# Cross-attention and gated FFN on one core: the V projection made straight behind K, the first half of U ahead of tile 2's scores, and inputs laid out by partition

## What is computed

```
q = (layernorm(x) @ Wq) * s ; k = (context @ Wk) * s ; v = context @ Wv        # s = 128 ** -0.25
attn = softmax(q @ k.T, per head) ; x = x + (attn @ v) @ Wo + bo
n = layernorm(x) ; shared = relu(n @ Ws1)**2 @ Ws2
logits = n @ Wr ; rw = softmax(top 2 of logits) ; prob = trunc(rw placed on the experts)
routed = sum over experts of prob * (relu(n @ W1[e])**2 @ W2[e])
x = x + shared + routed
```

## Time and profile before

| what | value |
|---|---|
| median of 3 runs | 116.21 us |
| the profiled execution | 116.54 us |
| its span, first to last instruction | 114.7 us |
| PE busy | 109.2 us (95%) |
| DVE, ACT, POOL busy | 87.6, 85.9, 65.5 us |
| PE's granted clock, mean | 0.996 |
| read from HBM, written | 8.42 MB, 2.10 MB |

### The profile page before, as it was taken

The page is one execution under the profiler, slowest core; times in us unless marked ns, Lnnn a source line. Parts: engine busy times, 40 slices in busy tenths (PEclk is TensorE's granted clock), DMA queues, the critical chain, the costliest instruction groups (busy, mean ns, idle before and its releaser), DMA issues.

```text
span 114.7 us, 3118 instructions
## 1 busy us (share of the span) xinstructions
PE 109.2 (95%) x854; PEld 105.8 (92%) x854; DVE 87.6 (76%) x349; ACT 85.9 (75%) x349; POOL 65.5 (57%) x106
## 2 busy tenths in 40 slices
PE   6987999999999989999999999999999999999991
PEld 6975999899998989999999999999999999989980
DVE  1019888569889697797979797987979786979973
ACT  4006926997948979898988889898989888997330
POOL 2005735956372965785676578657856766259341
PEclk9999999999999999999999999999999999999998
DMA  2899999995000200031005000400400050013034
GB/s 55 256 334 364 357 352 352 348 348 184 1 6 0 91 0 3 6 130 53 0 0 183 0 0 24 159 0 0 150 33 0 0 183 3 0 61 122 0 137 137
DMA packets 11815, 12.70 MB, mean 111 GB/s; under 512 B 1056, under 2 KB 10272, under 8 KB 11808
## 3 DMA queue, kind: packets, MB, share of 16 engines
q1 hardware_dynamic: 11520, 12.36, 32.4%
q10 hardware_dynamic: 288, 0.26, 0.7%
HBM read 8.42 MB, written 2.10 MB: 92 GB/s over the span
## 4 chain that ended last, share of the span: by engine, by line
PE 76%; DVE 7%; ACT 6%; DMA 4%; SPq 2%; issue 2%; POOL 1%; ACTq 0%; DVEq 0%
PE o_ps L432 8%; PE o_ps L434 7%; PE o_ps L433 7%; PE s_ps L432 7%; PE s_ps L434 7%; PE s_ps L433 7%; PE g_ps L492 6%; DMA wqt_sb<-in_wq_t 4%; PE f_ps L522 4%; ACT probs L710 4%; PE g_ps L505 3%; PE f_ps L432 2%; PE g_ps L446 2%; PE s_ps L622 1%; DVE wq_mean L1079 1%
## 5 line engine op out<-in xcount | busy, mean ns | idle before, releaser
L710 ACT ACTIVATE probs<-s_ps,neg_max,rstd 128x77 f32<-128x77 f32 x112 | 45.4, 428 | 4.0 <-DVE neg_max L950 4.0
L840 POOL TENSOR_TENSOR probs<-probs,recip 128x308 f32<-128x308 f32 x27 | 19.0, 703 | 23.5 <-DVE recip L956 23.4
L710 ACT ACTIVATION_READ_ACCUMULATOR probs<-s_ps,neg_max,rstd 128x1 f32 x112 | 24.2, 216 | 0.0
L432 PE MATMUL o_ps<-u_hi,pt_hi 128*128 128x256 f32 (+1 forms) x80 | 22.7, 284 | 0.2 <-DVE pt_lo L961 0.2
L434 PE MATMUL o_ps<-u_lo,pt_hi 128*128 128x256 f32 (+1 forms) x80 | 22.4, 280 | 0.0
L433 PE MATMUL o_ps<-u_hi,pt_lo 128*128 128x256 f32 (+1 forms) x80 | 22.4, 280 | 0.0
L432 PE MATMUL s_ps<-a_hi,xt_hi 128*128 128x308 f32 x64 | 22.1, 345 | 0.0
L434 PE MATMUL s_ps<-a_lo,xt_hi 128*128 128x308 f32 x64 | 19.4, 303 | 0.0
L433 PE MATMUL s_ps<-a_hi,xt_lo 128*128 128x308 f32 x64 | 19.4, 303 | 0.0
L432 PEld LDWEIGHTS o_ps<-u_hi,pt_hi 128*128 128x128 f32 (+1 forms) x80 | 15.0, 188 | 0.6 <-DVE pt_lo L961 0.6
L433 PEld LDWEIGHTS o_ps<-u_hi,pt_lo 128*128 128x128 f32 (+1 forms) x80 | 15.1, 188 | 0.0
(11 more groups left out here) (190 smaller groups left out, 270.8 us busy)
## 6 DMA issues: line engine op xcount, KB each, us to landing
xt_sb<-in_x_t SPq DMA_DIRECT2D x8, 256.0 KB, 6.7
x_sb<-in_x SPq DMA_DIRECT2D x8, 256.0 KB, 6.7
x_sb<-x_tr SPq DMA_DIRECT2D x7, 256.0 KB, 2.3
out<-y_sb SPq DMA_DIRECT2D x6, 256.0 KB, 2.3
wqt_sb<-in_wq_t SPq DMA_DIRECT2D x4, 256.0 KB, 5.0
wo_sb<-in_wo SPq DMA_DIRECT2D x1, 1024.0 KB, 9.0
wk_sb<-in_wk_p SPq DMA_DIRECT2D x3, 256.0 KB, 3.1
wv_sb<-in_wv_p SPq DMA_DIRECT2D x2, 384.0 KB, 6.2
```

What stands on the lines that cost most here:

```text
L432: pe.matmul(out_ap, hi, rhs_hi, start=first, stop=False)
L710: e = act.activation(probs_of(t)[:, par, h * TK:(h + 1) * TK], s_ps[:, 2 * par + half, (h - half * H // 2) * TK:(h - half * H // 2 + 1) * TK],
L840: pool.tensor_tensor(rows, rows, recip[:, par, hs].unsqueeze(2).broadcast_to([P, H // 2, TK]), ALU.mult).then_inc(probs_ready, 1)
```

## The change

Three things are changed. On PE, V's products stand straight behind K's, before A; half of U's products (heads 0 to 3) stand ahead of tile 2's scores, the other half behind them; and the first of U's transposes stands ahead of tile 0's transposition. ACT's and DVE's copies follow that order. On SP, Wv is loaded ahead of Wq. And the inputs are laid out by partition on the host, so that most loads read one piece of 2, 4 or 8 KB for each partition where they read pieces of 1 to 3 KB, and there are fewer loads: 21 in place of 32.

```diff
-            for i in range(2):
-                sp.dma_start(wk_sb[:, i, 0:HG, :].rearrange("p e c -> p (e c)"), wk_p[:, i, 0:HG * P]).then_inc(wk_in[i], 16)
...
+            def load_context_weights(w_sb, w_p, main_in, tail_in):
+                sp.dma_start(w_sb[:, 0:H, :], w_p[:, 0:H, :]).then_inc(main_in, 16)
+                sp.dma_start(w_sb[:, H:WT, :], w_p[:, H:WT, :]).then_inc(tail_in, 16)
...
+            sp.dma_start(ctx_sb[:, :, :], ctx_p).then_inc(ctx_in, 16)
+            load_context_weights(wk_sb, wk_p, wk_in, wk_tail_in)
+            load_context_weights(wv_sb, wv_p, wv_in, wv_tail_in)
             for i in range(4):
-                load_wq(i)
...
+                sp.dma_start(wqt_sb[:, 2 * i:2 * i + 2, :], wq_p[:, 2 * i:2 * i + 2, :]).then_inc(wq_in[i], 16)
             load_x_t(0)
             load_x(0)
...
-            load_wv(0)
-            load_wv(1)
...
@@ A: heads 4 to 7 write the banks that V's copies free @@
                     if h < H // 2:
                         pe.wait_ge(kt_copied, h + 1)
+                    else:
+                        pe.wait_ge(vt_copied, h - H // 2 + 1)
...
@@ PE's order @@
+            context_main(wk_sb, wk_in, s_banks)
+            context_tails(wk_sb, wk_tail_in, s_banks, kt_ready)
+            context_main(wv_sb, wv_in, once_banks)
+            context_tails(wv_sb, wv_tail_in, once_banks, vt_ready)
             make_a()
...
             scores(1, 1)
-            pe.wait_ge(wsr_ready, 1)
-            for i in range(2):
-                context_main(wv_sb, i, wv_in[i], once_banks)
-            context_tails(wv_sb, once_banks, vt_ready)
+            make_ut(0, H // 2)
             scores(2, 0)
-            make_ut()
+            make_ut(H // 2, H)
             pe.wait_ge(const_ready, 4)
+            make_u(0, 0)
             pe.wait_ge(exp_done, 5)
             transposes_x1(0, 0, transposes(0, 0))
-            for b, i in ((0, 0), (1, 0), (0, 1), (1, 1)):
+            for b, i in ((1, 0), (0, 1), (1, 1)):
...
@@ DVE @@
+            keep_ut(0)
+            keep_ut(1)
             reciprocals(0, 0, 0)
+            keep_ut(2)
+            keep_ut(3)
             reciprocals(0, 0, 1)
             maxima(2, 0)
             neg_maxima(2, 0)
...
+            reciprocals(1, 1, 0)
+            for h in range(4, H):
+                keep_ut(h)
+            reciprocals(1, 1, 1)
+            lo_of_u(0, 0)
             lo_of_transposes(0, 0)
```

More of the change, by code:

```diff
@@ L65, in program @@
     HALFP = P // 2
-    assert WB == HG + 2 and HG == 4
+    assert WT == H + 4 and HG == 4
     PB = (KC - 1) * P
@@ L396, in _, with context_main, context_tails @@
         def _(pe):
-            def context_main(w, i, w_in, banks):
+            def context_main(w, w_in, banks):
                 pe.wait_ge(w_in, 16)
-                for j in range(HG):
-                    h = HG * i + j
-                    pe.matmul(banks[h // 2][:, (h % 2) * BK:(h % 2 + 1) * BK], w[:, i, j, :], ctx_sb[:, 0, :],
+                for h in range(H):
+                    pe.matmul(banks[h // 2][:, (h % 2) * BK:(h % 2 + 1) * BK], w[:, h, :], ctx_sb[:, 0, :],
                               start=h % 2 == 0, stop=False)
-            def context_tails(w, banks, ready):
+            def context_tails(w, w_in, banks, ready):
+                pe.wait_ge(w_in, 16)
                 for i in range(2):
@@ L434, in three, with make_ut @@
                 return pe.matmul(out_ap, hi, rhs_lo, start=False, stop=last)
-            def make_ut():
-                for h in range(H):
+            def make_ut(first, end):
+                for h in range(first, end):
                     if h == 0:
                         pe.wait_ge(wo_in, 16)
-                    if h < H // 2:
-                        pe.wait_ge(vt_copied, h + 1)
-                    else:
+                    if h == 0:
+                        pe.wait_ge(wsr_ready, 1)
+                    if h >= H // 2:
                         pe.wait_ge(ut_copied, h - H // 2 + 1)
@@ L740, in _ @@
                                ACT.Copy, scale=SCALE2).then_inc(kt_copied, 1)
-                if g == 0:
-                    centre_wq(0, 2)
+            centre_wq(0, 2)
+            for g in range(H // 2):
+                act.wait_ge(vt_ready, g + 1)
+                act.activation(vt_sb[:, 2 * g:2 * g + 2, :].rearrange("p h n -> p (h n)"), once_banks[g][:, 0:2 * BK],
+                               ACT.Copy).then_inc(vt_copied, 1)
             centre_wq(4, 8)
@@ L751, in _ @@
             exps(0, 0, 1)
-            for g in range(H // 2):
-                act.wait_ge(vt_ready, g + 1)
-                act.activation(vt_sb[:, 2 * g:2 * g + 2, :].rearrange("p h n -> p (h n)"), once_banks[g][:, 0:2 * BK],
-                               ACT.Copy).then_inc(vt_copied, 1)
             exps(1, 1, 0)
@@ L758, in _ @@
             exps(2, 0, 0)
+            hi_of_u(0, 0)
             copy_transposes(0, 0)
-            for b, i in ((0, 0), (1, 0), (0, 1)):
+            for b, i in ((1, 0), (0, 1)):
                 hi_of_u(b, i)
@@ L1131, in _ @@
             step(1, 1, TG)
[L1132 to L1133 removed]
+            dve.wait_ge(x_in[2], 16)
+            dve.wait_ge(x_in[3], 16)
             with dve.Fori(1, (TILES - TG) // 2) as j:
```

111 lines of the change are left out of this document (45 added, 66 removed).

## The result

The changed kernel took 117.18 us (median of 20 runs, 116.62 to 118.13) against 116.44 (20 runs of the kernel before on the same chip): ratio 1.0074, 95% interval [1.0057, 1.0092]. It is slower by 0.7%, and outside the range of 115.4 to 116.8. The profiled execution took 117.23 us with a span of 115.4; 116.40 was forecast for it. All ratios leave out executions more than 1.5% above the fastest of the same kernel: one of experiment 5, three of experiment 10, and two of the kernel before beside experiments 9 and 10.

The account below looks back on a forecast made before the run. PE's stream was taken as the bound, capped by ACT: PE gains 1.95 us but gets 1.8 us of new waits; transposition +0.30, one transpose group -0.44, together -0.14 us, median 116.1 us. Range 115.4 to 116.8.

Parts of the forecast that it names:

- it stays there if the Wk load is there: Start of PE's work: K's first pass stays at 4.78 us, behind the warming up, provided Wk has landed.
- I take 9.2 and cost the load at nothing: Wq's first sum on DVE, behind Wv's 786 KB: taken at 9.2 us, between 8.8 and 10.4, at no cost.
- gaps of 1.95 us: PE's waits before K's tails and A's heads 0 and 2: V fills them, 1.48 of its 3.43 us remain.
- K without its wait for the tails ends at 4.78 + 3.43: PE's stream before A: K ends at 8.21 us, taking V's duration of 3.43 us, and V ends at 11.64.
- `neg_max` of tile 2: DVE, between tile 2's maxima (25.1 us) and its first exponential (26.3): starts 0.91 us after the maxima, at 26.0.
- V's 3.43 us: V's products on PE, placed between K and A: 3.43 us from first pass to the next work's first.
- Wq's first sum before 9.6: Sign on DVE: scores follow this sum by 6.24 us, so the load becomes the bound only after 9.60 us.
- The first window of the loads near 400 GB/s: Sign on the load queue: its first window of loads moves about 400 GB/s.
- The 0.44 us of one U group less behind it: PE behind tile 0's transposition: one group of U's transposes moved ahead, saving 0.44 us.
- Rival 3: Wk's larger load lands after 4.78 us, delaying everything up to the scores; 0.4 us late gives 116.5 us. Chance 0.1.
- Rival 1: Wq's load decides: first piece at 10.4 us, scores at 16.6, +0.63 us against before, 116.8 us. Chance 0.2.
- Rival 2: The new waits cost less, PE's 1.95 us come through in large part; half gives 115.2 us. Chance 0.18 above 0.58 us gain.

Follow-up runs that it names:

- experiment 5: Kernel before with one edit: Wv's two loads ahead of Wq's, order of work unchanged. 119.75 us, ratio 1.0273.
- experiment 10: Old order with larger loads, K's and V's products from first halves of context and Wk's main rows, Wv late and unused. 117.47 us, ratio 1.0086.
- experiment 9: Changed kernel, K's and V's products from first halves of context and Wk's main rows, Wv unused, POOL's tile 3 splitting later. 116.86 us, ratio 1.0052.
- experiment 6: Changed kernel with V computed from Wk's tile, Wv loaded late and unused, context and Wk loads cut as before. 117.39 us, ratio 1.0112.
- experiment 7: Changed kernel, V from Wk's tile, Wv late, first loads cut, and POOL's splitting of tile 3's x behind tile 1's first normalisation. 117.37 us, ratio 1.0087.
- experiment 4: Changed kernel with POOL's splitting of tile 3's x moved behind the first normalisation of tile 1. 117.05 us, ratio 1.0063.
- experiment 1: Changed kernel with its first two loads, context and Wk's main part, cut in two each as before. 117.82 us, ratio 1.0121.
- experiment 3: Kernel before with the new order of work and Wv loaded ahead of Wq, keeping its small loads and layout. 117.93 us, ratio 1.0133.
- experiment 11: Changed kernel's order, K and V from first halves of context and Wk's main rows, Wq's pieces loaded directly behind those. 116.61 us, ratio 1.0027.
- experiment 8: Kernel before's order with new layout and larger loads, Wk's main rows in halves, Wq's first piece ahead of Wk's tail. 116.29 us, ratio 1.0003.
- experiment 2: Changed kernel's layout and larger loads alone, in the kernel before's order of work and loads. 116.59 us, ratio 1.0021.

## Why the prediction was wrong

**The step that failed** is "it stays there if the Wk load is there", with "I take 9.2 and cost the load at nothing, its cover being PE's own work on K and V". I read the slump of the earlier trace rows as the work of two small loads and took it to vanish with larger ones. It stayed (199 and 258 GB/s in the changed kernel, 160 and 176 in experiment 6). So the loads of K itself are late, by an amount that changes from run to run (K's first pass at 5.18, 4.98 and 5.42 us in three traces with Wk's main rows in one load). PE's own work was to cover the loads, but the cover is counted from K's start, and that start hangs on a load. The gaps of 1.95 us had been the slack of this stage: 0.55 of them was such a wait for Wk, and a longer one would have gone out of the wait for Wq behind it. The change filled the slack with V, so every wait for a load in front of V counts in full. The rows of before hint at it: the second of Wk's two halves, issued at 1.6 us, took 3.1 us to land, at 4.7, against K's start at 4.78. One load for both halves had less than 0.1 us to spare; it landed at 5.0.

**What the sum left out** is the clock. "K without its wait for the tails ends at 4.78 + 3.43" takes PE at its full level from K's first product on, which is what one trace showed. In experiment 7 it was not until 7.3 us, and K and the warming up took 1.47 us more. In the old order the 1.95 us of gaps cover that; the sum gave them to V. The profiled execution of the changed kernel did not pay this, so its 0.91 us are the load, V and `neg_max`; in the median it is probably a part of the miss (116.98 against 117.18, an estimate from the table above).

**The term that was mis-sized**: `neg_max` of tile 2, 0.23 us in the sum and 0.60 measured, since POOL's subtraction now falls upon it (experiment 4). In the profiled execution that is 0.37 of the 0.91 us; in the medians experiment 4 gives 0.13 us and experiment 7 against 6 some 0.3 (1.0112 - 1.0087), neither clear of its interval. V's 3.43 us, which measured 3.53, is a smaller such term. The prediction had POOL's copies in view only as a bound on A, and never asked what they would now run beside.

**Point by point.** K's tails without a wait: right. A without a gap: right, but at 12.22, not near 11.6. K and V 6.86 us: 7.04. A 4.20: right. Wq's first sum before 9.6: 9.70, a tenth beyond, without effect as PE was later still. First exponential 19.7: 20.30. The first window of the loads near 400 GB/s: wrong, 289 at 3 to 4 us and 199 at 4 to 5; it was 406 only at 9 to 10. `row_max` of tile 2 near 25.1: 25.72, by the late scores. Idle of 1.1 us before tile 2's scores: 1.09. Standstill of 0.7 before the transposition: 0.57, with the transposes of U hidden in front of it. The 0.44 us of one U group less behind it: the way from the transposition to tile 3's scores was to fall from 2.65 to 2.21 and fell to 2.27. The Trainium skill's limit ("DMA: Bandwidth & Descriptors", Specifications) of about 358 GB/s was again exceeded, by the 433 of the window, and yet the first sum (9.70) lay nearer to the 9.9 that I had estimated from the page's figure than to my 9.2: for the slump, not for the rate.

**The rivals.** Rival 3 (K late) is what the changed kernel's trace shows, with the 0.4 us that its text names; it prices that at 116.5, or 116.8 for the profiled execution (116.54 + 0.26); that one took 117.23, and `neg_max` makes up most of the rest. Rival 1 stands directly behind it: where K was early, the late Wv and Wq decided (experiments 1 and 3). I gave the two 0.3 together, as if one excluded the other; they are one cause, the load queue in its first 10 us, and should have had well over half. A late rise of the clock was no rival at all. Rival 2 had nothing for it.

**Still open.** How much of the 0.7% is late loads and how much a late clock: experiment 11 has nothing left to wait for in its trace, yet its runs go from 116.05 to 117.63. The late clock fits this spread, but only a trace of one of its slow executions would show it. Neither was it told why the queue slumps at 4 to 7 us; it does so with large and with small rows.

No version that computes the whole reference beat the kernel before; experiments 8 (1.0003) and 2 (1.0021) can't be told from it.

## What to carry to other kernels

A gap that you fill was also a buffer: before you put work into it, list every earlier wait that ended inside it, for each will count in full afterwards. A load in the first microseconds is not to be priced by the steady rate of the queue; take the time at which it lands from a trace, with its spread over runs. Such a gap also absorbs what changes from execution to execution, such as the moment at which PE's clock rises: a sum taken from one trace can't show that, so sort the times of many executions before you trust it. And "covered by the engine's own work" holds only if that work starts without a load of its own.
